# All four quarters of the expert up weights split, GpSimd forms the fourth remainder

## The chip, the cores and the metric

The kernel runs on one core of one Trainium2 chip. The metric is the device time in microseconds of one execution; a shorter time is better. Its engines are TensorE (PE in the profile, with its weight loads as PEld), VectorE (DVE), ScalarE (ACT), GpSimd (POOL) and SyncE (SP). Each runs its own list of instructions in order, and they wait for one another by semaphores.

## What is computed

Two graph layers with a dense part each, on 1250 nodes of 512 features. The change touches only the last part, a mixture of 16 experts of which each node uses 2:

```python
cw = jnp.sum(jax.nn.one_hot(idx, E) * w[..., None], axis=1)        # top-2 weights of each node
he = jnp.einsum('nd,edh->enh', xf, expert_w1) + expert_b1[:, None, :]
te = swiglu5(he, ...)                                               # clip, sigmoid, products
oe = jnp.einsum('enh,ehd->end', te, expert_w2) + expert_b2[:, None, :]
y = jnp.einsum('ne,end->nd', cw, oe)
```

`expert_w1` is 512 x 768 for each expert, `expert_w2` 384 x 512. All of it is float32.

## The kernel before

The 2500 node-expert assignments are sorted by expert and cut into **blocks** of 128 rows that belong to one expert; with this input there are 28 blocks, numbered 0 to 27. Each block b goes through these steps. Blocks come in pairs, an even one (buffer k = 0) and an odd one (k = 1), and pair i holds blocks 2i and 2i+1. Pairs 3 to 13 are a loop on every engine.

- **SP** loads the expert's weights into WB, five buffers deep, and only where the expert changes.
- **POOL** `gather` (L653, L656): copies the block's row numbers to `idx`, and an indirect DMA fetches its 128 rows into `xg[k]`. It waits until the rows of block b-2 have been transposed (`xt_ps`).
- **PE** `turn_rows` (L1356): four transposes of the gathered rows into PSUM bank 4.
- **ACT** `rows_hi`: copies the fourth quarter (128 of the 512 features) as plain float32 to `xgf` (L965), and rounds the three others to fp32r as XGH (L966). **DVE** `rows_lo` (L1998) forms their remainder XGL.
- **ACT** `split_hi` (L976), once for each half h of the 768 columns: rounds three quarters (FR = 3) of the up weights to fp32r as W1H. **DVE** `split_lo` (L2006) forms the remainder W1L of each half. The semaphore `w1_hi` counts the halves of ACT.
- **PE** `up`: for each half one float32 product for the fourth quarter (L1372, two records in the profile), and for each of the three others the three fp32r products high x high, low x high, high x low (L1378, nine records).
- **DVE** `units` and **ACT** `sigmoid` (L942): bias, clipping, the gated unit. **PE** `turn_act` (L1387) and **ACT** `turn_t` (L935): its transpose.
- **PE** `down` (L1425): three float32 products with `expert_w2`. **ACT** `result` (L951): scales the block's rows into `yo[k]`; for block b it waits until the scatter of block b-2 has landed, which read the same buffer (`scattered`).
- **POOL** `scatter` (L667, L672): a copy of the destinations, and an indirect DMA that adds the 128 rows into the output. Its copy waits for the landing of the scatter in front of it.

The order on each engine is written out by hand in `pair(i)`. PE: `turn_rows(2i)`, `down(2i-3)`, `up(2i-1)` with `turn_act(2i-2)` between its halves, `turn_rows(2i+1)`, `down(2i-2)`, `up(2i)`. ACT: `rows_hi(2i)`, `sigmoid(2i-2)`, `split_hi(2i)` half 0, `result(2i-3)`, `split_hi(2i)` half 1, `turn_t(2i-2)`, and then the same for the odd block, with `split_hi(2i+1)` half 0, `result(2i-2)`, `split_hi(2i+1)` half 1. POOL: `gather(2i)`, `scatter(2i-5)`, `gather(2i+1)`, `scatter(2i-4)`; the gathers of blocks 0 to 3 stand ahead of that, and five scatters behind the loop.

Before the experts, ACT stores the finished output rows of the shared part in three stores (`store`, the first one of HEAD node tiles), since W1H and W1L of the odd buffer lie where those rows lay.

Of the kernel before, what the change touches and what calls it, by code (L numbers as in the profile page):

```python
# [14 lines left out]
ALU = mybir.AluOpType  # L15
# [8 lines left out]
D = 512  # L24
# [3 lines left out]
FT = D // 128  # L28
# [50 lines left out]
INTER = 384  # L79
H2 = 2 * INTER  # L80
# [4 lines left out]
WBUF = O_B1 + H2  # L85
EARLY = NT
NWB = 5
# [5 lines left out]
ASSIGN = TOPK * NT  # L93
LENT = (1, 3, 5, 7)
AHEAD = 5
HEAD = 5
FR = 3
WIDE = ((0, 112), (112, NP))


def build(nc, a, out):
    ctx = ExitStack()
    with ctx:
# [3 lines left out]
        def sem(name):  # L107
            return ctx.enter_context(nc.semaphore(name))

        PS = ctx.enter_context(nc.psum_tensor("PS", [128, 8, 512], F32))  # L110
# [59 lines left out]
        f32 = lambda m: m.bitcast(F32)  # L170
# [5 lines left out]
        YF = at("YF", R_YH, [128, NT * D])  # L176
        RT = at("RT", R_YL, [128, NT * D])
        QX = at("QX", R_XN, [128, NT * D])
        WB = at("WB", R_ZH, [128, NWB * WBUF])
# [127 lines left out]
        w1_in = [sem("w1_in0"), sem("w1_in1")]  # L307
        w2_in = [sem("w2_in0"), sem("w2_in1")]
        xt_ps, xgt_ready = sem("xt_ps"), sem("xgt_ready")
        xgt_hi, xgt_f, w1_hi, w1_lo, out_head = sem("xgt_hi"), sem("xgt_f"), sem("w1_hi"), sem("w1_lo"), sem("out_head")  # L310
        hb_ready, clip_done, clip_g, gate_sig, t_gs, t_ready = (
            sem("hb_ready"), sem("clip_done"), sem("clip_g"), sem("gate_sig"), sem("t_gs"), sem("t_ready"))
        clip_u = sem("clip_u")
# [5 lines left out]
        out_stored = sem("out_stored")  # L319
# [42 lines left out]
        W1H = [at("W1H0", R_XN + 8192, [128, FR, H2], F32R), at("W1H1", R_X, [128, FR, H2], F32R)]  # L362
        W1L = [at("W1L0", R_YL + ROWB - W1B, [128, FR, H2], F32R), at("W1L1", R_X + W1B, [128, FR, H2], F32R)]
        XGH = at("XGH", R_YH + 4096, [128, 2, FR, 128], F32R)
        XGL = at("XGL", R_YL + 4096, [128, 2, FR, 128], F32R)
        xgf = YF[:, 1792:2048].rearrange("p (b n) -> p b n", b=2)

        rat = [2 * INTER]

# [43 lines left out]
        eb_i = sb("eb_i", [1, 4, NB], I32)  # L413
# [129 lines left out]
        def _(pool):  # L543
# [105 lines left out]
            def gather(i, k, b):  # L649
                if not (isinstance(b, int) and b < 2):  # L650
                    pool.wait_ge(xt_ps, b - 1)
                turn = b + 1 if isinstance(b, int) else pool.to_reg(b + 1)
                pool.tensor_copy(idx[:, k:k + 1], tok[:, bass.ds(b, 1)]).then_inc(idx_ready, 1)  # L653
                pool.wait_ge(xn_stored, 32)
                pool.wait_ge(idx_ready, turn)
                pool.indirect_dma_start(xg[:, k, :], None, xn_dram[:, :],  # L656
                                        bass.IndirectOffsetOnAxis(idx[:, k:k + 1], 0)
                                        ).then_inc(gathered[k], 16)

            def scatter(k, b):  # L660
                if isinstance(b, int):
                    turn, seen = b + 1, 16 * b
                else:
                    turn, seen = pool.to_reg(b + 1), pool.to_reg(b * 16)
                if not (isinstance(b, int) and b < 1):
                    pool.wait_ge(scattered, seen)
                pool.tensor_copy(dest_i[:, k:k + 1], home[:, bass.ds(b, 1)]).then_inc(dest_ready, 1)  # L667
                pool.wait_ge(out_head, 32)
                pool.wait_ge(out_stored, 64)
                pool.wait_ge(yo_ready, turn)  # L670
                pool.wait_ge(dest_ready, turn)
                pool.indirect_dma_start(out[:, :], bass.IndirectOffsetOnAxis(dest_i[:, k:k + 1], 0), yo[:, k, :], None,  # L672
                                        compute_op=ALU.add).then_inc(scattered, 16)

            for b in range(4):
                gather(0, b % 2, b)
            pool.wait_ge(zeroed, 16)
            last = last_pair(pool)

            def pair(i):  # L680
                gather(i, 0, i * 2)
                if not (isinstance(i, int) and i * 2 < AHEAD):
                    scatter(1, i * 2 - AHEAD)
                gather(i, 1, i * 2 + 1)
                scatter(0, i * 2 + 1 - AHEAD)

            pair(2)
            with pool.Fori(3, NB // 2) as i:
# [9 lines left out]
        def _(act):  # L698
# [66 lines left out]
            n = 0  # L765
# [196 lines left out]

            def rows_hi(k, b):
                act.wait_ge(xt_ps, b + 1)
                nc.scalar.copy(xgf[:, k, :], PS[:, 4, FR * 128:D]).then_inc(xgt_f, 1)  # L965
                nc.scalar.copy(XGH[:, k, :, :], PS[:, 4, 0:FR * 128].rearrange("p (f n) -> p f n", f=FR)  # L966
                               ).then_inc(xgt_hi, 1)

# [50 lines left out]
        def _(pe):  # L1019
# [33 lines left out]
            for b in range(NBAT):  # L1053
# [6 lines left out]
                for j in range(PER):  # L1060
# [5 lines left out]
                    for x in range(OWN):  # L1066
                        mm = nc.tensor.matmul(windows(b)[:, :, place], oh_lo[b % RING][0:CHUNK, j, :, x],  # L1067
                                              oh_key[b % RING][0:CHUNK, j, :, x].rearrange("p (t w) -> p t w", t=NT),
                                              start=False, stop=(j == PER - 1 and x == OWN - 1 and b == NBAT - 1))
# [38 lines left out]
            for t in range(NT):  # L1108
                mm = nc.tensor.matmul(PS[0:NP, 3, t:t + 1], invc[0:1, t * NP:(t + 1) * NP], ones[0:1, 0:1],
                                      start=True, stop=True)  # L1110
# [61 lines left out]
            for pos in range(POS):  # L1172
                for t in range(NT):
                    i = pos * NT + t
# [175 lines left out]
            def turn_rows(i, k, b):  # L1350
                pe.wait_ge(gathered[k], i * 16 + 16)
                if not (isinstance(b, int) and b < 1):
                    pe.wait_ge(xgt_ready, b)
                    pe.wait_ge(xgt_f, b)
                for f in range(FT):
                    mm = nc.tensor.transpose(PS[:, 4, f * 128:(f + 1) * 128], xg[:, k, f * 128:(f + 1) * 128], ident[:, :])  # L1356
                mm.then_inc(xt_ps, 1)
# [3 lines left out]
                    pe.wait_ge(clip_done, p - 1)  # L1361

            def up(k, b, between):
                off = pe.value_load(eb_i[0:1, 1, bass.ds(b, 1)], min_val=0, max_val=(NWB - 1) * WBUF)
                pe.wait_ge(xgt_f, b + 1)
                up_bank_free(b)
                for h in range(2):
                    if h and between:
                        between()
                    cols = slice(h * INTER, (h + 1) * INTER)  # L1370
                    pe.wait_ge(w1_lo, b * 2 + (h + 1))
                    nc.tensor.matmul(PS[:, 2 * k + h, 0:INTER], xgf[:, k, :],  # L1372
                                     WB[:, bass.ds(off + (FR * H2 + h * INTER), INTER)], start=True, stop=False)
                    if h == 0:
                        pe.wait_ge(xgt_ready, b + 1)
                    for f in range(FR):
                        for j, (x, wt) in enumerate(((XGH, W1H), (XGL, W1H), (XGH, W1L))):
                            mm = nc.tensor.matmul(PS[:, 2 * k + h, 0:INTER], x[:, k, f, :], wt[k][:, f, cols],  # L1378
                                                  start=False, stop=(f == FR - 1 and j == 2))
                mm.then_inc(hb_ready, 1)  # L1380

            def turn_act(k, p):
# [102 lines left out]
        def _(dve):  # L1485
# [515 lines left out]
            def split_lo(k, b, h):  # L2001
                off = dve.value_load(eb_i[0:1, 1, bass.ds(b, 1)], min_val=0, max_val=(NWB - 1) * WBUF)
                cols = slice(h * INTER, (h + 1) * INTER)
                dve.wait_ge(w1_hi, b * 2 + (h + 1))
                raw = WB[:, bass.ds(off, FR * H2)].rearrange("p (f n) -> p f n", f=FR)
                v.tensor_tensor(W1L[k][:, :, cols], raw[:, :, cols], f32(W1H[k][:, :, cols]), ALU.subtract  # L2006
                                ).then_inc(w1_lo, 1)

            def units(k, b, then):
# [204 lines left out]
```

## Time and profile before

| | us |
|---|---|
| median of 3 runs | 865.25 (862.41 to 865.94) |
| the profiled execution | 863.68 |
| its span, first to last instruction | 861.7 |
| busy in the span: PE | 792.2 (92%) |
| PE weight loads | 618.9 (72%) |
| DVE | 528.1 (61%) |
| ACT | 321.1 (37%) |
| POOL | 139.2 (16%) |

The stage of the experts runs from about 620 us of the span to its end. The profile gives each instruction's line, start and duration, which engine or DMA ended the idle time in front of it, the chain of waits that ended last, and the clock that TensorE was granted as a share of its full speed. Several records of one line are merged there, and the count is given as x4 or x9.

### The profile page before, as it was taken

The page shows a single profiled execution, that of the slowest core. Times are in us where ns is not written, and L with a number is a line of the kernel's source. Part 1 is how long each engine was busy: PE and PEld are TensorE (multiplying, and loading weights), DVE is VectorE, ACT ScalarE, POOL GpSimd, SP SyncE. Part 2 cuts the span into 40 slices and gives each one's busy share as a digit, 9 for nine tenths or more (in the row PEclk, how much of TensorE's full clock was granted, in tenths as well). Part 3 has the DMA queues.
Part 4 walks back from the last instruction along what each step waited for, and adds up shares of the span by engine and source line. Part 5 has one row for each costly group of instructions (what it writes and reads, how often), then busy time and mean ns, then how long its engine had stood idle before and what let it go on. Part 6 is the DMA issues. An engine that isn't in the chain of part 4 may idle for free.

```text
span 861.7 us, 13555 instructions
## 1 busy us (share of the span) xinstructions
PE 792.2 (92%) x3933; PEld 618.9 (72%) x3934; DVE 528.1 (61%) x943; ACT 321.1 (37%) x542; POOL 139.2 (16%) x186
## 2 busy tenths in 40 slices
PE   3899899999999989997999969988989999999983
PEld 1556788888888876676888857877867777777761
DVE  7787832421441487887023675897487878778751
ACT  1563512521431204533211253332255555556531
POOL 2000000000000210000000500212134343545321
PEclk9999899999999998998999998987999999999997
DMA  7500000000000010000101103002998949874632
GB/s 173 162 1 2 1 1 1 1 0 1 1 1 1 31 52 0 1 1 1 49 1 45 72 2 120 1 0 90 335 339 271 312 94 361 268 201 73 155 60 35
DMA packets 32292, 71.39 MB, mean 83 GB/s; under 512 B 4387, under 2 KB 4637, under 8 KB 32243
## 3 DMA queue, kind: packets, MB, share of 16 engines
q1 hardware_dynamic: 24480, 53.31, 17.8%
q0 software_dynamic: 6272, 14.68, 8.5%
q10 hardware_dynamic: 1491, 2.73, 0.9%
q8 instruction: 32, 0.52, 0.2%
q14 instruction: 17, 0.14, 0.0%
HBM read 96.53 MB, written 12.72 MB: 127 GB/s over the span
## 4 chain that ended last, share of the span: by engine, by line
PE 77%; DVE 15%; issue 4%; ACT 2%; DMA 1%; DVEq 1%; ACTq 0%; POOL 0%; POOLq 0%
PE PS L1125 22%; PE PS L1159 10%; PE PS L1378 9%; PE PS L1425 8%; PE PS L1257 5%; PE PS L1067 4%; PE PS L1372 4%; PE PS L1200 3%; PE PS L1410 3%; PE PS L1049 2%; PE PS L1356 1%; PE PS L1387 1%; PE PS L1098 1%; DVE XN L1495 1%; PE PS L1302 1%
## 5 line engine op out<-in xcount | busy, mean ns | idle before, releaser
L1125 PE MATMUL PS<-CTR,YH 125*128 125x500 f32 (+1 forms) x480 | 164.4, 358 | 2.3 <-DVE YL L1683 2.3
L1125 PE MATMUL PS<-CTR,YL 125*128 125x500 f32 (+1 forms) x480 | 163.8, 356 | 0.0
L1125 PEld LDWEIGHTS PS<-CTR,YH 125*128 125x128 f32 x480 | 91.6, 191 | 15.6 <-DVE YL L1683 2.6
L1125 PEld LDWEIGHTS PS<-CTR,YL 125*128 125x128 f32 x480 | 91.8, 191 | 13.0
L2006 DVE TENSOR_TENSOR W1L<-WB,W1H 128x1152 fp32r<-128x1152 f32 x56 | 74.0, 1356 | 17.1 <-issue 10.1
L1425 PE MATMUL PS<-WB,YF 128*128 x168 | 78.6, 605 | 2.5 <-issue 1.7
L1710 DVE TENSOR_TENSOR ZL<-PS,ZH 128x500 fp32r<-128x500 f32 (+1 forms) x36 | 21.1, 591 | 90.4 <-ACT ZH L789 90.4
L1378 PE MATMUL PS<-W1H,XGH 128*128 128x384 f32 x168 | 73.2, 436 | 0.0
L976 ACT CAST W1H<-WB 128x1152 fp32r x56 | 64.2, 1151 | 16.3 <-issue 11.0
L1378 PE MATMUL PS<-W1L,XGH 128*128 128x384 f32 x168 | 57.3, 341 | 0.0
L1378 PE MATMUL PS<-W1H,XGL 128*128 128x384 f32 x168 | 56.9, 339 | 0.0
L789 ACT CAST ZH<-PS 128x500 fp32r<-128x500 f32 (+1 forms) x36 | 18.1, 508 | 97.5 <-PE PS L1125 97.5
L672 POOL DMA_INDIRECT out<-YF,dest_i x28 | 48.3, 1727 | 35.1 <-ACT YF L951 20.2
L1425 PEld LDWEIGHTS PS<-WB,YF 128*128 128x128 f32 x168 | 30.2, 193 | 30.4 <-issue 30.4
L1372 PE MATMUL PS<-WB,YF 128*128 x112 | 45.5, 488 | 2.4 <-DVE W1L L2006 2.4
L1159 PE MATMUL PS<-WH,ZH 128*125 128x512 f32 x120 | 47.3, 394 | 0.0
L1159 PE MATMUL PS<-WL,ZH 128*125 128x512 f32 x120 | 47.3, 394 | 0.0
L1159 PE MATMUL PS<-WH,ZL 128*125 128x512 f32 x120 | 47.2, 394 | 0.0
L1067 PE MATMUL PS<-ET 125*128 125x120 f16 x330 | 44.0, 309 | 2.1 <-issue 2.1
L566 POOL MEMSET FMASK<- 128x1 f32 x1 | 0.1, 98 | 283.0 <-PE PS L1125 283.0
L1721 DVE SCALAR_TENSOR_TENSOR tmp<-PS,dis,bias 125x512 f32<-125x512 f32 x30 | 22.5, 751 | 35.7 <-PE PS L1159 35.7
L1067 PEld LDWEIGHTS PS<-ET 125*128 125x128 f16 x330 | 30.5, 135 | 18.3 <-issue 17.4
(393 smaller groups left out, 1638.9 us busy)
## 6 DMA issues: line engine op xcount, KB each, us to landing
WB<-in_w SPq DMA_DIRECT2D x28, 1536.0 KB
WB<-in_w SPq DMA_DIRECT2D x28, 768.0 KB
WB<-in_b SPq DMA_DIRECT2D x28, 384.0 KB
X<-in_x SPq DMA_DIRECT2D x1, 2240.0 KB
xn_dram<-XN SPq DMA_DIRECT2D x1, 2240.0 KB
WNEXT<-in_W SPq DMA_DIRECT2D x2, 1024.0 KB, 10.1
SR<-in_sw SPq DMA_DIRECT2D x1, 1536.0 KB, 7.7
out<-X ACTq DMA_DIRECT2D x1, 1120.0 KB
```

What stands on the lines that cost most here:

```text
L672: pool.indirect_dma_start(out[:, :], bass.IndirectOffsetOnAxis(dest_i[:, k:k + 1], 0), yo[:, k, :], None, compute_op=ALU.add).then_inc(sca ...
L976: nc.scalar.copy(W1H[k][:, :, cols], raw[:, :, cols]).then_inc(w1_hi, 1)
L1067: mm = nc.tensor.matmul(windows(b)[:, :, place], oh_lo[b % RING][0:CHUNK, j, :, x], oh_key[b % RING][0:CHUNK, j, :, x].rearrange("p (t w) ...
L1125: mm = nc.tensor.matmul(dest, lhs, rhs, start=(t == 0 and h == 0), stop=(t == NT - 1 and h == 1))
L1159: mm = nc.tensor.matmul(PS[0:NP, 6 + n % 2, :], z[:, f, t * NP:(t + 1) * NP], w[:, f, :], start=(f == 0 and h == 0), stop=(f == FT - 1 and ...
L1200: mm = nc.tensor.matmul(PS[0:TILE[j], 3 + j, 0:RC], w[rows, k, cols], x, start=(k == tiles[0] and h == 0), stop=(k == 2 and h == 2))
L1257: mm = nc.tensor.matmul(PS[:, 4 + n % 4, 0:w], wt[:, f, fo * 128:(fo + 1) * 128], z[:, f, c0:c0 + w], start=(f == 0 and h == 0), stop=(f = ...
L1372: nc.tensor.matmul(PS[:, 2 * k + h, 0:INTER], xgf[:, k, :], WB[:, bass.ds(off + (FR * H2 + h * INTER), INTER)], start=True, stop=False)
L1378: mm = nc.tensor.matmul(PS[:, 2 * k + h, 0:INTER], x[:, k, f, :], wt[k][:, f, cols], start=False, stop=(f == FR - 1 and j == 2))
L1410: nc.tensor.matmul(PS[0:NP, bank, :], x[:, c, nodes], wt[:, c, :], start=(c == 0 and j == 0), stop=False)
L1425: mm = nc.tensor.matmul(PS[:, 6 + k, :], tt[:, k, j, :], WB[:, bass.ds(off + (O_W2 + j * D), D)], start=(j == 0), stop=(j == 2))
L2006: v.tensor_tensor(W1L[k][:, :, cols], raw[:, :, cols], f32(W1H[k][:, :, cols]), ALU.subtract).then_inc(w1_lo, 1)
```

## The change

HEAD goes from 5 to 6 and FR from 3 to 4: ACT rounds all four quarters of the rows and of the weights (512 instead of 384, and 1536 instead of 1152 elements of each partition), and the separate copy `xgf` with its semaphore is gone. DVE forms the remainder of all four quarters of the rows, and of three quarters of the weights as before. The remainder of the weights' fourth quarter, 768 elements of each partition, is formed by POOL in a new step, `split_rest`, which waits for both halves of ACT's rounding of that block and raises `w1_rest`. PE replaces the float32 product by three fp32r ones and waits for `w1_rest` ahead of the last product of each half.

```diff
-HEAD = 5
-FR = 3
+HEAD = 6
+FR = FT
...
+            def split_rest(k, b):
+                off = pool.value_load(eb_i[0:1, 1, bass.ds(b, 1)], min_val=0, max_val=(NWB - 1) * WBUF)
+                pool.wait_ge(w1_hi, b * 2 + 2)
+                pool.tensor_tensor(W1L[k][:, FR - 1, :], WB[:, bass.ds(off + (FR - 1) * H2, H2)],
+                                   f32(W1H[k][:, FR - 1, :]), ALU.subtract).then_inc(w1_rest, 1)
+
             for b in range(4):
                 gather(0, b % 2, b)
+            split_rest(0, 0)
+            pool.wait_ge(out_stored, 64)
+            for b in range(1, 4):
+                split_rest(b % 2, b)
             pool.wait_ge(zeroed, 16)
...
                     scatter(1, i * 2 - AHEAD)
                 gather(i, 1, i * 2 + 1)
+                split_rest(0, i * 2)
                 scatter(0, i * 2 + 1 - AHEAD)
+                split_rest(1, i * 2 + 1)
...
             def rows_hi(k, b):
                 act.wait_ge(xt_ps, b + 1)
-                nc.scalar.copy(xgf[:, k, :], PS[:, 4, FR * 128:D]).then_inc(xgt_f, 1)
...
                     pe.wait_ge(w1_lo, b * 2 + (h + 1))
-                    nc.tensor.matmul(PS[:, 2 * k + h, 0:INTER], xgf[:, k, :],
-                                     WB[:, bass.ds(off + (FR * H2 + h * INTER), INTER)], start=True, stop=False)
...
                         for j, (x, wt) in enumerate(((XGH, W1H), (XGL, W1H), (XGH, W1L))):
+                            if f == FR - 1 and j == 2:
+                                pe.wait_ge(w1_rest, b + 1)
...
-                v.tensor_tensor(W1L[k][:, :, cols], raw[:, :, cols], f32(W1H[k][:, :, cols]), ALU.subtract
+                v.tensor_tensor(W1L[k][:, 0:FR - 1, cols], raw[:, :, cols], f32(W1H[k][:, 0:FR - 1, cols]), ALU.subtract
```

The place on POOL is the second half of a pair in the loop. Before, from the wait of the second gather to the branch back:

```order
L652 ISA [waits xt_ps]
L653 COPY idx<-tok 128x1
L656 DMA YF<-xn_dram,idx 128x512 [waits idx_ready,xn_stored]
L664 ISA
L667 ISA [waits scattered]
L667 COPY dest_i<-RT 128x1
L672 DMA out<-YF,dest_i 1378x512 [waits yo_ready,dest_ready,out_stored,out_head]
L689 UNCONDITIONAL_BRANCH
```

In the changed kernel the same gather is followed by these rows; W1L_109 is the remainder of the even buffer, W1L_110 that of the odd one, and the row behind the last is the branch back to the next pair's gather:

```order
L678 ISA [waits w1_hi]
L678 TENSOR_TENSOR W1L_109<-WB,W1H_107 128x768
L664 ISA
L667 ISA [waits scattered]
L667 COPY dest_i<-RT 128x1
L672 DMA out<-YF,dest_i 1378x512 [waits yo_ready,dest_ready,out_stored,out_head]
L676 ISA
L676 TENSOR_LOAD eb_i
L676 ISA x2
L677 ISA
L678 ISA [waits w1_hi]
L678 TENSOR_TENSOR W1L_110<-WB,W1H_108 128x768
```

Two waits for ACT's `w1_hi` now stand in POOL's list, one ahead of the second scatter and one ahead of the next pair's two gathers.

On PE the place is one half of `up`. Before:

```order
L1372 ISA [waits w1_lo,clip_done,xgt_f]
L1372 MATMUL PS<-WB,YF 128x384
L1378 MATMUL PS<-W1H_107,XGH 128x384 [waits xgt_ready]
L1378 MATMUL PS<-W1H_107,XGL 128x384
L1378 MATMUL PS<-W1L_109,XGH 128x384
L1378 MATMUL PS<-W1H_107,XGH 128x384
L1378 MATMUL PS<-W1H_107,XGL 128x384
L1378 MATMUL PS<-W1L_109,XGH 128x384
L1378 MATMUL PS<-W1H_107,XGH 128x384
L1378 MATMUL PS<-W1H_107,XGL 128x384
L1378 MATMUL PS<-W1L_109,XGH 128x384
```

And in the changed kernel:

```order
L1386 MATMUL PS<-W1H_107,XGH 128x384 [waits xgt_ready,w1_lo,clip_done]
L1386 MATMUL PS<-W1H_107,XGL 128x384
L1386 MATMUL PS<-W1L_109,XGH 128x384
L1386 MATMUL PS<-W1H_107,XGH 128x384
L1386 MATMUL PS<-W1H_107,XGL 128x384
L1386 MATMUL PS<-W1L_109,XGH 128x384
L1386 MATMUL PS<-W1H_107,XGH 128x384
L1386 MATMUL PS<-W1H_107,XGL 128x384
L1386 MATMUL PS<-W1L_109,XGH 128x384
L1386 MATMUL PS<-W1H_107,XGH 128x384
L1386 MATMUL PS<-W1H_107,XGL 128x384
L1386 MATMUL PS<-W1L_109,XGH 128x384 [waits w1_rest]
```

The float32 product is gone, twelve fp32r products stand where there were nine, and the last of them waits for POOL.

## Rows read from the trace of the kernel before

**Rows 1.** The page's chain that ended last, share of the span by engine.

```profile
PE 77%; DVE 15%; issue 4%; ACT 2%; DMA 1%; DVEq 1%; ACTq 0%; POOL 0%; POOLq 0%
```

**Rows 2.** The chain of waits over blocks 4 and 5: start us, us, what.

```profile
642.93 0.44 PE PS L1356 x4
643.37 2.58 PE PS L1425 x6
645.95 0.65 PE PS L1372 x2
646.59 1.57 PE PS L1378 x9
648.16 0.33 PE PS L1387 x3
...
650.71 0.44 PE PS L1356 x4
```

**Rows 3.** Stretches: us, busy us (and count) by engine, clock, DMA share, GB/s.

```profile
640.00:820.00 180.00, 180.00 (x814) 133.09 (x812) 144.38 (x186) 104.66 (x163) 78.71 (x89) 1.00 0.75 223
846.00:850.00 4.00, 4.00 (x6) 1.22 (x5) 0.00 (x0) 0.00 (x0) 0.59 (x2) 0.57 0.52 66
```

**Rows 4.** Timeline of POOL, 704 to 713: start, us, instruction, [idle before].

```profile
704.43 1.85 POOL L672 DMA_INDIRECT out<-YF,dest_i  x1 [0.83 <-POOL dest_i L667]
705.77 0.71 POOL L653 COPY idx<-tok 128x1 int32 x1
707.26 1.17 POOL L656 DMA_INDIRECT YF<-xn_dram,idx  x1 [0.77 <-POOL idx L653]
709.64 0.18 POOL L667 COPY dest_i<-RT 128x1 int32 x1 [1.22 <-DMA out<-YF,dest_i]
711.11 1.62 POOL L672 DMA_INDIRECT out<-YF,dest_i  x1 [1.28 <-ACT YF L951]
```

**Rows 5.** Lines L656 (gather) and L672 (scatter): their count and their landing.

```profile
L656 POOL DMA_INDIRECT YF<-xn_dram,idx x28: 967/1114/2002, 602.4 to 807.9; - x28
DMA to landing us min/median/max: 3.4/5.7/6.8
...
L672 POOL DMA_INDIRECT out<-YF,dest_i x28: 1561/1673/2173, 640.5 to 852.0; - x28
DMA to landing us min/median/max: 4.6/5.1/9.0
```

**Rows 6.** Groups by line and shape: POOL's two long subtractions, busy us, mean ns.

```profile
L614 POOL TENSOR_TENSOR SL<-SR,SH 128x3072 fp32r<-128x3072 f32 x1 | 6.8, 6831 | 0.0
L616 POOL TENSOR_TENSOR SL<-SR,SH 128x1536 fp32r<-128x1536 f32 x1 | 3.5, 3499 | 0.0
```

**Rows 7.** Timeline of ACT for block 3.

```profile
635.79 0.48 ACT L966 CAST XGH<-PS 128x384 fp32r<-128x384 f32 x1
637.13 0.65 ACT L942 ACTIVATE bias<-bias,acts 128x384 f32<-128x384 f32 x1 [0.85 <-DVE bias L2023]
637.84 1.15 ACT L976 CAST W1H<-WB 128x1152 fp32r x1
638.90 0.68 ACT L951 ACTIVATE YF<-PS,wslot 128x512 f32<-128x512 f32 x1
639.48 1.15 ACT L976 CAST W1H<-WB 128x1152 fp32r x1
```

**Rows 8.** Timeline of POOL and DVE in the shared part, around 556 and 560.

```profile
556.11 1.26 POOL L643 TENSOR_TENSOR TL<-ST,TH 128x500 fp32r<-128x500 f32 x1 [12.66 <-ACT TH L915]
556.95 0.96 DVE L1942 SCALAR_TENSOR_TENSOR ST<-SG,SC,ST 128x500 f32<-128x500 f32 x1
...
560.25 0.78 DVE L1942 SCALAR_TENSOR_TENSOR ST<-SG,SC,ST 128x500 f32<-128x500 f32 x1
```

**Rows 9.** Timeline of the last block: its down product, its scatter.

```profile
845.73 4.53 PE L1425 MATMUL PS<-WB,YF 128*128 x6 [0.72 <-ACT YF L935]
...
852.00 1.57 POOL L672 DMA_INDIRECT out<-YF,dest_i  x1 [1.94 <-ACT YF L951]
```

More of the change, by code:

```diff
@@ L309, in build @@
         xt_ps, xgt_ready = sem("xt_ps"), sem("xgt_ready")
-        xgt_hi, xgt_f, w1_hi, w1_lo, out_head = sem("xgt_hi"), sem("xgt_f"), sem("w1_hi"), sem("w1_lo"), sem("out_head")
+        xgt_hi, w1_hi, w1_lo, out_head = sem("xgt_hi"), sem("w1_hi"), sem("w1_lo"), sem("out_head")
+        w1_rest = sem("w1_rest")
         hb_ready, clip_done, clip_g, gate_sig, t_gs, t_ready = (
@@ L365, in build @@
         XGL = at("XGL", R_YL + 4096, [128, 2, FR, 128], F32R)
-        xgf = YF[:, 1792:2048].rearrange("p (b n) -> p b n", b=2)
         rat = [2 * INTER]
@@ L1353, in turn_rows @@
                     pe.wait_ge(xgt_ready, b)
-                    pe.wait_ge(xgt_f, b)
                 for f in range(FT):
@@ L1363, in up @@
             def up(k, b, between):
-                off = pe.value_load(eb_i[0:1, 1, bass.ds(b, 1)], min_val=0, max_val=(NWB - 1) * WBUF)
-                pe.wait_ge(xgt_f, b + 1)
                 up_bank_free(b)
@@ L1377, in up @@
                         for j, (x, wt) in enumerate(((XGH, W1H), (XGL, W1H), (XGH, W1L))):
+                            if f == FR - 1 and j == 2:
+                                pe.wait_ge(w1_rest, b + 1)
                             mm = nc.tensor.matmul(PS[:, 2 * k + h, 0:INTER], x[:, k, f, :], wt[k][:, f, cols],
-                                                  start=False, stop=(f == FR - 1 and j == 2))
+                                                  start=(f == 0 and j == 0), stop=(f == FR - 1 and j == 2))
                 mm.then_inc(hb_ready, 1)
@@ L2004, in split_lo @@
                 dve.wait_ge(w1_hi, b * 2 + (h + 1))
-                raw = WB[:, bass.ds(off, FR * H2)].rearrange("p (f n) -> p f n", f=FR)
-                v.tensor_tensor(W1L[k][:, :, cols], raw[:, :, cols], f32(W1H[k][:, :, cols]), ALU.subtract
+                raw = WB[:, bass.ds(off, (FR - 1) * H2)].rearrange("p (f n) -> p f n", f=FR - 1)
+                v.tensor_tensor(W1L[k][:, 0:FR - 1, cols], raw[:, :, cols], f32(W1H[k][:, 0:FR - 1, cols]), ALU.subtract
                                 ).then_inc(w1_lo, 1)
```

## The prediction

> **What bounds the kernel now.** I read the page's chain first: 77% of the span lies on PE [rows 1]. Then the chain over two blocks of the stage that the change touches [rows 2]. It is PE without a gap: four transposes 0.44, the down product 2.58, a half of `up` 0.65 + 1.57, the transposes of the activation 0.33, and the other half 0.65 + 1.57. From one block's transposes to the next one's are 650.71 − 642.93 = 7.78 us. The stage's sums say the same: PE is busy for all of 180 us at full clock, DVE for 144 and ACT for 105 of them [rows 3]. So the stage is bound by PE, and everything else must only be in time. The reader should then ask how much in time POOL is, since the change gives it new work with new waits. POOL's timeline [rows 4] has the gather of block b start 1.7 us behind the end of the transposes of block b−2 (642.93 + 8 × 7.78 + 0.44 = 705.6, then 707.26), and its landing takes 5.7 us by the median [rows 5]. The rows are needed 15.56 − 0.44 = 15.1 us after they were allowed to be fetched, so POOL may be 15.1 − 1.7 − 5.7 = 7.7 us later than now before PE waits.
>
> **PE's part.** A half of `up` loses the float32 product, 0.65, and gains three fp32r products at 1.57/9 = 0.174 each, 0.52: 0.13 less for each half, 0.25 for each block, 7 us for 28 blocks. PE's period becomes 7.53. That is what the change brings if PE stays the bound.
>
> **ACT's and DVE's part.** ACT's cast of 384 elements takes 0.48 and that of 1152 takes 1.15 [rows 7], 0.87 ns an element, so the two casts of a block take 1.48 instead of 1.15, and that of the rows 0.59. The copy `xgf` goes. ACT gains about half a microsecond a block and DVE 0.1, and both have over 1.5 us of idle time a block [rows 3]; as work this costs nothing. But the end of the second cast now releases POOL. HEAD moves one tile of output from the second store into the first: the same bytes, taken as nothing, with 1 us either way.
>
> **POOL's part.** `split_rest` subtracts 768 elements. POOL's two long subtractions give (6831 − 3499)/1536 = 2.17 ns an element [rows 6], 1.67, and 0.08 behind ACT's semaphore: 1.75 us. As work that would fit beside the 79 us in 180 of now. What matters is the wait. `split_rest(2i+1)` stands ahead of the branch back, so ahead of `gather(2i+2)`, and it waits for ACT to round block 2i+1, which ACT starts only when PE has transposed the rows of 2i+1. But PE needs `gather(2i+2)` just one period after that. So the gather loses all its lead: what was issued a period ahead is now issued when the block in front is half done.
>
> I follow the loop from A, the end of the transposes of block 2i, all in us:
>
> 1. ACT: rounds the rows, then (rows 7 for the starts: 637.13 to 637.84 is 0.71, to 638.90 is 1.06) the sigmoid, half 0 and `result(2i−3)`. It would reach that at 0.05 + 0.52 + 0.71 + 1.06 + 0.33 = 2.7 (the 0.52 is the 0.59 less its overlap with the next). But the down product in front of it runs on a PE that has waited for many microseconds. After the waits at the end of the program the granted clock was 0.57 of the full 2.4 GHz, so mostly at the level of 1.2 GHz, and this same down took 4.53 [rows 3, 9]. So `result` starts at 4.5, half 1 at + 0.58, and ends at + 1.48: **6.6**.
> 2. POOL: `split_rest(2i)`, **1.75**.
> 3. POOL: `scatter(2i−4)`: the copy and its wait 1.0 [rows 4], and the landing: median 5.1, largest 9.0 [rows 5]. Weight loads are issued behind each `down`, thus about now, and I take 6.3: **7.3**. Its landing counts since ACT's `result(2i−2)` waits for it, and half 1 of the odd block stands behind that `result`. By here A + 15.6 is reached. PE's way to the same point: 4.4 (cold down) + 2 × 2.09 + 0.33 + 0.44 = 9.4 to the next transposes, and ACT 3.6 to `result`: 13.0. So the scatter is later, not PE.
> 4. ACT: `result` and half 1: 0.15 + 0.58 + 1.48 = **2.2**.
> 5. POOL: `split_rest(2i+1)`, **1.75**.
> 6. POOL: `gather(2i+2)`: copy 0.18, then 0.76 until the DMA [rows 4], the landing 3.4 to 6.8 [rows 5]; the queues are rather quiet at this point, so below the median: 4.4. Four transposes take 0.44 warm and twice that at half the clock, 0.8: **6.15**.
>
> The sum is 6.6 + 1.75 + 7.3 + 2.2 + 1.75 + 6.15 = 25.75 us for a pair, where now it is 15.56. The gather of 2i+1 is issued behind one scatter and is in time (about A + 4 against A + 9).
>
> **The whole.** Block 3: its transposes end at 635.6 and ACT's second cast at 640.6 [rows 7], now 0.66 later, and `split_rest(3)` ends at 643.05. Then `gather(4)`, here beside weight loads (5.7 instead of 4.4): the transposes of block 4 end at 650.5 instead of 643.4. Eleven pairs later, block 26: 650.5 + 11 × 25.75 = 933.7. Steps 1 to 5 follow once more (19.6) to 953.3; then five scatters in a row, each 1.0 + 5.1, since only now POOL comes to them: the last one's DMA starts 0.3 (reading the loop's end, an estimate) + 1.0 + 4 × 6.1 later, at 979.0. In the profile 9.7 us lie between that point and the end [rows 9], so the span is 988.7. The profiled execution is 2.0 above its span, 863.68, and the median of the runs 1.6 above it: 992 us. That the 7 us on PE don't show is part of this: PE waits 8 to 9 us in each pair (25.75 − 0.8 − 9.4 − 7.1).
>
> **The bounds of the unknown costs.** Below: a landing of 3.4 for the gather and 4.6 for the scatter and no loss of clock: 4.95 + 1.75 + 5.6 + 2.2 + 1.75 + 4.95 = 21.2 a pair, 942 in all. Above: landings of 5.7 and 9.0 and the rival on the port below in full: 25.75 + 1.3 + 2.7 + 2.7 = 32.5, 1066 in all. All at one end is unlikely.
>
> **The rivals.**
>
> *POOL and DVE hold each other up.* `split_rest` and the DVE's `split_lo` of half 1 wait for the same semaphore. In the shared part, a DVE instruction with two inputs from SBUF took 0.96 when it began under a subtraction of POOL, and 0.78 otherwise [rows 8]. If the DVE's 1.36 goes first, POOL starts 1.35 later, twice a pair: 28.45, and 11 × 2.7 = 30 us more, 1022. For it: both engines are idle and waiting there. Against it: POOL started 0.08 behind ACT in the shared part, the DVE about 0.16, and where POOL goes first it is DVE that waits, which costs nothing. 20%. The Trainium skill, SBUF — State Buffer, section "Who interferes with whom", states the rule: such a DVE instruction and a GpSimd instruction that reads SBUF exclude each other, and whichever is first holds the port for its whole length. The 0.18 us of the rows agrees with that, but shows only DVE as the one that waits.
>
> *The scatter is off the chain.* If it lands before PE's way arrives (within 3.7 us of its issue, under the least of 4.6, or with PE colder for longer), the pair is 9.4 + 3.6 + 0.58 + 1.48 + 1.75 + 6.15 = 22.95, and the time 961. 12%.
>
> *PE stays the bound, the change is faster.* It needs `gather(2i+2)` issued within the 7.7 us of slack. The last step ahead of it must then end 7.53 − 0.44 − 0.94 − 5.7 = 0.45 us after the odd block's transposes. The time would be 865 − 7 = 858. For it: PE is the only bound now, and POOL has the time as a sum. Against it: ACT's second cast alone ends 640.6 + 0.66 − 635.6 = 5.7 us after those transposes, and the list of POOL leaves no other way around. 3%.
>
> **The chances.** The loop as written 62%, the port 20%, the scatter off the chain 12%, PE bound 3%, and 3% for something else, a part of it near the time of now. Faster by over 0.5% (which is what a measurement of this kernel can tell from no change) 3%, within it 1%, slower 96%. The range for 8 in 10: the loop with landings about a microsecond off either way is 11 × 2 = 22 on either side, the two neighbouring cases lie at 961 and 1022: 950 to 1045.
>
> **What would show it.** In the profile after: PE idle for 8 to 9 us ahead of every even block's transposes from block 4 on, and the wait ends by the gather's DMA; the clock below 1.00 behind each of these waits; POOL's `split_rest` behind idle time that ACT's cast ended; ACT's `result` of the even blocks waiting for the scatter's DMA; the `up` halves at 12 × 0.174 = 2.09; 24 to 28 us between the transposes of blocks 2i and 2i+2; POOL's subtraction at 1.7, and at 3 where the port decides. The prediction is wrong if PE runs through, or if the gather of an even block starts ahead of the casts of the block in front of it.

## The result, and the profile after

| | before | after |
|---|---|---|
| median of 3 runs | 865.25 us | 1016.25 us (1015.67 to 1018.85) |
| profiled execution / its span | 863.68 / 861.7 us | 1016.25 / 1014.5 us |
| mean granted clock of PE | 0.967 | 0.903 |

The changed kernel takes 1.178 times as long [1.1755, 1.1806]: 151 us more. 992 us was predicted, in a range of 950 to 1045.

The page's chain that ended last, of the changed kernel (share of the span by engine), stands against [rows 1]:

```profile
PE 56%; DVE 12%; DMA 12%; issue 11%; ACT 5%; POOLq 1%; POOL 1%; ACTq 1%; SPq 0%; DVEq 0%
```

PE falls from 77% to 56%; DMA goes from 1% to 12%, and "issue" from 4% to 11%. The stage was PE without a gap [rows 2]; now its chain runs over DMAs. The same chain over one pair of blocks (start us, us, what; the short pieces between these are left out) shows its links:

```profile
707.24 1.11 PE PS L1366 x4
708.42 4.47 PE PS L1433 x6
713.07 0.30 ACT YF L963
713.79 1.49 ACT W1H L987
715.66 2.76 issue
718.42 0.19 POOL dest_i L667
719.42 5.92 DMA out<-YF,dest_i
725.45 0.29 ACT YF L963
726.16 1.48 ACT W1H L987
728.41 2.33 issue
730.74 0.19 POOL idx L653
731.72 3.40 DMA YF<-xn_dram,idx
735.24 1.11 PE PS L1366 x4
```

The links are, in order: cold transposes and a cold down product on PE (cold means at a lowered clock), ACT's `result` and cast, a hole of 2.76, POOL's scatter, ACT's `result` and cast again, a hole of 3.1 (727.64 to 730.74), POOL's gather, and PE. From transposes to transposes are 28.0 us, where two blocks took 15.56 before [rows 2]. The holes are POOL's `split_rest`, of which the chain names only 0.09 and calls the rest "issue"; the timelines of DVE and POOL do (start, us, instruction, [idle before and what ended it]):

```profile
715.42 1.36 DVE L2014 TENSOR_TENSOR W1L<-WB,W1H 128x1152 fp32r<-128x1152 f32 x1 [1.99 <-ACT W1H L987]
715.46 3.02 POOL L678 TENSOR_TENSOR W1L<-WB,W1H 128x768 fp32r<-128x768 f32 x1 [6.13 <-ACT W1H L987]
...
727.77 1.36 DVE L2014 TENSOR_TENSOR W1L<-WB,W1H 128x1152 fp32r<-128x1152 f32 x1 [4.46 <-ACT W1H L987]
727.81 2.98 POOL L678 TENSOR_TENSOR W1L<-WB,W1H 128x768 fp32r<-128x768 f32 x1 [6.78 <-ACT W1H L987]
```

Both engines waited for the same cast, DVE begins 0.04 ahead, and POOL's 768 elements take 3.0, not 1.75. The line's group has it for all blocks (min/median/max ns):

```profile
L678 POOL TENSOR_TENSOR W1L<-WB,W1H x28: 1845/2994/3022, 615.7 to 976.0; 128x768 fp32r<-128x768 f32 x28
```

The view of waits from 620 to the end (engine and line, what it waited for: total us, times, longest) reads the same way from the other side:

```profile
POOL W1L L678 <- ACT W1H L987: 174.1, 27, 8.7
...
PE PS L1366 <- DMA YF<-xn_dram,idx: 117.1, 12, 11.6
...
ACT YF L963 <- DMA out<-YF,dest_i: 43.5, 13, 4.8
```

PE loses 117.1 us in twelve waits for the gather of an even block, 10.3 in the one ahead of 735.24, and more by its clock. Of the stretches (us, busy us and count of PE, PEld, DVE, ACT, POOL, clock, DMA share, GB/s) the first answers to [rows 3], the second is the down product behind such a wait:

```profile
660.00:820.00 160.00, 96.96 (x405) 70.91 (x403) 72.21 (x91) 58.29 (x66) 67.47 (x58) 0.80 0.52 150
708.40:712.80 4.40, 4.38 (x7) 1.98 (x8) 2.66 (x4) 2.68 (x3) 0.93 (x1) 0.63 0.48 106
```

PE is busy 61% where it was busy all the time, no other engine is above 46%, and the DMA engines are at 52%: nothing is the bound by its work.

### The profile page after: what moved, and what is told of

Same layout as the page of the kernel before. It is cut to its first block, busy times and chain, and to the rows that moved or that the text cites. A ratio compares the mean times of both kernels' runs of the same rounds, so it can differ in the third digit from the quotient of the medians.

```text
span 1014.5 us, 13638 instructions
## 1 busy us (share of the span) xinstructions
PE 817.3 (81%) x3989; PEld 639.6 (63%) x3990; DVE 535.0 (53%) x943; ACT 342.5 (34%) x514; POOL 207.7 (20%) x215
## 4 chain that ended last, share of the span: by engine, by line
PE 56%; DVE 12%; DMA 12%; issue 11%; ACT 5%; POOLq 1%; POOL 1%; ACTq 1%; SPq 0%; DVEq 0%
PE PS L1136 18%; PE PS L1170 8%; DMA out<-YF,dest_i 7%; PE PS L1433 6%; PE PS L1268 4%; DMA YF<-xn_dram,idx 4%; PE PS L1078 4%; ACT W1H L987 4%; PE PS L1386 3%; PE PS L1211 3%; PE PS L1418 2%; PE PS L1366 2%; PE PS L1060 1%; PE PS L1109 1%; DVE XN L1503 1%
## 5 line engine op out<-in xcount | busy, mean ns | idle before, releaser
L1366 PE MATMUL PS<-ident,YF 128*128 128x128 f32 x112 | 23.4, 346 | 117.1 <-DMA YF<-xn_dram,idx 117.1
L678 POOL TENSOR_TENSOR W1L<-WB,W1H 128x768 fp32r<-128x768 f32 x28 | 81.7, 2919 | 174.3 <-ACT W1H L987 174.1
L1433 PE MATMUL PS<-WB,YF 128*128 x168 | 99.9, 741 | 4.1 <-ACT YF L947 3.0
L1386 PE MATMUL PS<-W1H,XGH 128*128 128x384 f32 x224 | 90.2, 402 | 1.4 <-DVE W1L L2014 1.4
L987 ACT CAST W1H<-WB 128x1536 fp32r x56 | 82.4, 1477 | 15.3 <-issue 9.4
L1386 PE MATMUL PS<-W1L,XGH 128*128 128x384 f32 x224 | 76.7, 342 | 0.0
L1386 PE MATMUL PS<-W1H,XGL 128*128 128x384 f32 x224 | 76.1, 340 | 0.0
L2006 DVE TENSOR_TENSOR XGL<-PS,XGH 128x512 fp32r<-128x512 f32 x28 | 19.3, 688 | 63.0 <-ACT XGH L977 61.1
L672 POOL DMA_INDIRECT out<-YF,dest_i x28 | 45.3, 1618 | 23.2 <-POOL dest_i L667 22.4
L1386 PEld LDWEIGHTS PS<-W1H,XGH 128*128 128x128 f32 x224 | 43.5, 194 | 8.4 <-issue 6.8
L1386 PEld LDWEIGHTS PS<-W1H,XGL 128*128 128x128 f32 x224 | 43.3, 193 | 6.6 <-issue 6.6
```

What stands on the lines that cost most here:

```text
L678: pool.tensor_tensor(W1L[k][:, FR - 1, :], WB[:, bass.ds(off + (FR - 1) * H2, H2)], f32(W1H[k][:, FR - 1, :]), ALU.subtract).then_inc(w1_r ...
L987: nc.scalar.copy(W1H[k][:, :, cols], raw[:, :, cols]).then_inc(w1_hi, 1)
L1433: mm = nc.tensor.matmul(PS[:, 6 + k, :], tt[:, k, j, :], WB[:, bass.ds(off + (O_W2 + j * D), D)], start=(j == 0), stop=(j == 2))
```

## The experiments

Ratios are against the kernel before, run on the same chip (its medians were 863.6 to 864.6).

**1. The waits alone.** The kernel before, with nothing but the two waits in POOL's list:

```diff
                 gather(i, 1, i * 2 + 1)
+                pool.wait_ge(w1_hi, (i * 2) * 2 + 2)
                 scatter(0, i * 2 + 1 - AHEAD)
+                pool.wait_ge(w1_hi, (i * 2 + 1) * 2 + 2)
```

> The kernel before with nothing but two waits added to POOL's list in pairs 2 to 13, at the places where the changed kernel has its subtractions: for both halves of ACT's cast of block 2i ahead of the second scatter, and of block 2i+1 ahead of the branch back. No subtraction on POOL, no other cast, the float32 product stays. Theory (the waits, not the work, are the larger part): the gather of each even block is issued behind the cast of the block in front, PE waits ahead of it, the pair takes 20 to 21.5 us instead of 15.6, and the time is 920 to 945 us, about 935. That is roughly half of the loss of 151 us; the rest is 2 x 3.0 us of subtraction and the longer casts, which only count because they lie on this chain. Rival (a wait alone costs nothing while POOL has the time as a sum): 865 us.

Measured: 971.57 us (967.72 to 975.23), ratio 1.125 [1.1202, 1.1289]. Two waits with no work behind them cost 108 of the 151 us. That is the mechanism, but dearer than I expected: the pair shown below is 716.58 to 740.20, 23.6 us, and from block 6 to block 26 a pair takes 25.1 in the mean. POOL's timeline, with DVE and PE beside it, tells part of why:

```profile
725.06 1.36 DVE L2008 TENSOR_TENSOR W1L<-WB,W1H 128x1152 fp32r<-128x1152 f32 x1 [2.31 <-ACT W1H L978]
725.17 1.29 POOL L667 COPY dest_i<-RT 128x1 int32 x1 [6.54 <-ACT W1H L978]
...
735.02 0.77 POOL L653 COPY idx<-tok 128x1 int32 x1 [6.14 <-ACT W1H L978]
...
740.20 1.09 PE L1358 MATMUL PS<-ident,YF 128*128 128x128 f32 x4 [4.80 <-DMA YF<-xn_dram,idx]
```

The copy of one element a partition takes 1.29 when DVE's subtraction begins ahead of it, and ends 0.04 behind it; with DVE out of its way it takes 0.18 [rows 4] or 0.20, and 0.71 to 0.77 where it begins under a scatter's issue. The gather's copy of 0.77 above ends 0.05 behind another subtraction of DVE (734.38 to 735.74). PE then waits 4.8, and its record of four transposes is 1.09 long, where a warm one has 0.60 (of which 0.44 pass before the down product begins). The chain over this pair shows two more links that my expectation didn't name:

```profile
717.75 5.11 PE PS L1427 x6
...
727.29 4.98 DMA out<-YF,dest_i
```

They are the cold down product and the landing of the scatter, which also waits for a cast here.

**2. DVE behind POOL.** The changed kernel; DVE's half 1 waits for POOL's remainder of that block, so the two are never at it together.

```diff
+                if h and not (isinstance(b, int) and b < 2):
+                    dve.wait_ge(w1_rest, b + 1)
```

> The changed kernel, but DVE's subtraction of half 1 waits until POOL's subtraction of the same block is done (blocks 2 and later), so the two never overlap at that point. Theory (the port: DVE goes first for 1.36 us and POOL starts behind it): POOL's subtraction falls from 2.99 to 1.7 us, twice in each pair on the chain, the pair from about 28.0 to 25.4 us, the time by 26 x 1.3 = 33 us, to about 984 us. Rival (POOL's subtraction takes 2.99 us by itself with these operands, with or without DVE): 2.99 us stays and the time stays at 1016 us or above.

Measured: 997.79 us (996.71 to 1002.79), ratio 1.157 [1.1532, 1.1604]: 18 us less than the changed kernel, not 33. The duration of the term is settled by the line's group:

```profile
L678 POOL TENSOR_TENSOR W1L<-WB,W1H x28: 1792/1830/2047, 615.7 to 956.8; 128x768 fp32r<-128x768 f32 x28
```

1.83 for the same instruction on the same data, where the changed kernel has 2.99. The Trainium skill, SBUF — State Buffer, section "Who interferes with whom", has the rule for this: a DVE instruction with two inputs from SBUF and a GpSimd instruction that reads SBUF exclude each other, and the first one holds on for its whole length; here 1.16 us are added to the one that comes second, by a DVE instruction of 1.36. Pairs lie between 24.8 and 27.6, 26.1 in the mean, where I expected 25.4. The view of waits from 620 to 1000 has what changed beside POOL:

```profile
ACT bias L954 <- DVE bias L2033: 33.1, 14, 3.5
ACT YF L963 <- DMA out<-YF,dest_i: 3.1, 5, 1.4
```

ACT's wait for DVE's clip was 15.2 in the changed kernel, and its wait for the scatter 43.5: DVE comes later by its new wait. The chain over the pair from 701.46 to 728.45 has, beside that, a longer cold down product and a longer landing of the gather than the changed kernel's pair (4.47 and 3.40):

```profile
702.64 5.42 PE PS L1433 x6
...
724.30 4.02 DMA YF<-xn_dram,idx
```

How the missing 15 us divide between these isn't shown.

**3. The scatter ahead of the first remainder.** The changed kernel with two calls exchanged.

```diff
                 gather(i, 1, i * 2 + 1)
-                split_rest(0, i * 2)
                 scatter(0, i * 2 + 1 - AHEAD)
+                split_rest(0, i * 2)
                 split_rest(1, i * 2 + 1)
```

> The changed kernel with the pair's second scatter moved ahead of the first remainder in POOL's list, so it no longer waits for the cast of block 2i. Theory (the scatter's landing is a link of the chain, since ACT's result and behind it the second half of the odd block's cast wait for it): ACT's wait for the scatter goes, PE's way to the same point takes over 2 to 4.5 us earlier, the pair falls from about 28.0 to about 24 us, the time by 11 x 4.4 = 48 us, to about 968 us (960 to 990). Rival (the gather's lateness alone sets the pair, the scatter runs beside PE): no change, 1016 us.

Measured: 979.59 us (976.59 to 981.52), ratio 1.133 [1.1294, 1.1362]. ACT's wait for the scatter is all but gone,

```profile
ACT YF L963 <- DMA out<-YF,dest_i: 2.3, 2, 1.7
```

and a pair takes 24.7 in the mean from block 4 to block 26 (the shortest is 725.36 to 748.81, 23.5), where the changed kernel has 27.8. So the scatter behind the first remainder was a link of the chain (steps 2 and 3 of the prediction). That the way over PE is what remains in its place was expected, and isn't shown apart.

**4. Both casts ahead of `result`.** The changed kernel; in ACT's list `split_hi(i, 0, ..., 1)` stands ahead of `result(1, i*2−3)`, and the odd one likewise:

```diff
                 split_hi(i, 1, i * 2 + 1, 0)
-                result(0, i * 2 - 2)
                 split_hi(i, 1, i * 2 + 1, 1)
+                result(0, i * 2 - 2)
```

> The changed kernel itself (1016 us) with only ACT's order changed: both halves of the cast ahead of the result. POOL's list keeps its waits. Theory (the chain runs through down, result and the scatter's landing into the second half of the cast): w1_hi comes at about 4.2 instead of 6.9 us behind the transposes of an even block, the scatter's landing is no longer awaited ahead of the odd block's cast, and the pair falls to about 23.4 us: 965 us (955 to 985), with the gathers of even blocks still behind POOL's wait. Rival (only POOL's order matters): 1016 us.

Measured: 975.87 us (975.31 to 977.52), ratio 1.130 [1.125, 1.1339], within the 955 to 985 expected, with pairs of 24.4 in the mean: the cast that releases POOL no longer stands behind the cold down product and the scatter's landing. ACT's wait for the scatter falls from 43.5 to 11.4. Experiments 3 and 4 each take most of ACT's wait for the scatter away, and each leaves 111 to 116 us of the loss, near what the waits alone cost: the gather of the even block still stands behind the second cast of the block in front of it.

**5. The gathers ahead of the remainders.** Each pair forms the remainders of the two blocks in front of it, each behind one of its gathers and one of its scatters:

```diff
-            for b in range(1, 4):
-                split_rest(b % 2, b)
+            split_rest(1, 1)
...
                     scatter(1, i * 2 - AHEAD)
+                split_rest(0, i * 2 - 2)
                 gather(i, 1, i * 2 + 1)
-                split_rest(0, i * 2)
                 scatter(0, i * 2 + 1 - AHEAD)
-                split_rest(1, i * 2 + 1)
+                split_rest(1, i * 2 - 1)
...
                 scatter((j + 1) % 2, end + j)
+                if j < 2:
+                    split_rest(j, end + 3 + j)
```

> The changed kernel with POOL's list shifted: in pair i it forms the remainders of blocks 2i-2 and 2i-1 instead of 2i and 2i+1, each behind the gather of two blocks later, so that no gather stands behind a wait for the cast of the block in front of it. All of POOL's work stays, 28 subtractions. Theory (the order of the waits is the whole loss): PE runs without a gap again at 7.53 us a block instead of 7.78, gathers start about 1.7 us behind the transposes that free their buffer, and the time is 865 - 7 = 858 us (855 to 861). Rival (POOL's work and its hold on the port are the loss, 28 x 3.0 us of subtraction beside DVE): most of the loss stays, the time is over 930 us. Between: if the DVE, held up by POOL, comes too late with its half of the weights, PE has a short wait in each block and the time is 862 to 880.

Measured: 888.41 us (885.47 to 890.99), ratio 1.028 [1.0255, 1.0305]. All arithmetic of the change is still there, and the larger `HEAD` too, and 128 of the 151 us are gone: so much of the loss is one of order. But it is not faster than the kernel before. In the stretch of 160 us PE is idle for 15.6:

```profile
660.00:820.00 160.00, 144.39 (x667) 111.91 (x666) 128.19 (x145) 89.32 (x107) 101.14 (x91) 0.97 0.64 181
```

The timelines of POOL and DVE show one place:

```profile
688.75 1.60 POOL L672 DMA_INDIRECT out<-YF,dest_i  x1 [0.83 <-POOL dest_i L667]
689.82 2.40 POOL L678 TENSOR_TENSOR W1L<-WB,W1H 128x768 fp32r<-128x768 f32 x1
```

```profile
689.31 3.14 DVE L2032 TENSOR_SCALAR bias<-bias,clampv 128x384 f32<-128x384 f32 x1 [0.19 <-DVE bias L2029]
```

DVE's clip of 384 elements takes 0.48 elsewhere. Here it begins under POOL's issue of a scatter and ends at 692.45, 0.23 behind the end of POOL's subtraction; its mean is 1.05 from 641 to 840. The clip stands on the way to the next down product.

**6. DVE forms all four quarters.** POOL's list is that of before.

```diff
-                split_rest(0, i * 2)
-                split_rest(1, i * 2 + 1)
...
-                            if f == FR - 1 and j == 2:
-                                pe.wait_ge(w1_rest, b + 1)
...
-                raw = WB[:, bass.ds(off, (FR - 1) * H2)].rearrange("p (f n) -> p f n", f=FR - 1)
+                raw = WB[:, bass.ds(off, FR * H2)].rearrange("p (f n) -> p f n", f=FR)
```

> The changed kernel with the fourth quarter's remainder formed by DVE together with the others (1536 elements of each partition in each half instead of 1152), POOL's list as in the kernel before, no wait on POOL in PE's products. Theory (the waits in POOL's list are the loss): PE bound, 858 us. DVE gains 2 x 0.4 us a block and is busy for about 7.1 of 7.53 us; if its order leaves gaps at that load, PE waits a little and the time is up to 870. Rival (POOL's work costs): also fast, so this run alone does not part them. Rival (twelve fp32r products or the longer casts of ACT are the loss): stays near 1016.

Measured: 875.99 us (872.39 to 877.98), ratio 1.015 [1.0125, 1.0168]. The full computation of the change without POOL is the nearest to the kernel before. The stretch shows DVE at 137.5 of 160 us, 86% (80% in [rows 3]):

```profile
660.00:820.00 160.00, 150.26 (x719) 115.53 (x718) 137.53 (x156) 98.51 (x118) 75.86 (x80) 1.00 0.66 186
```

From block 6 on, blocks take 7.9 to 8.7 us, 8.3 in the mean, where 7.78 is to be beaten. That DVE's load is what holds them up is argued from its share, not shown.

**7. The gathers ahead, with a remainder of 32 columns.** As experiment 5, but POOL subtracts 32 columns instead of 768; the fourth quarter's product with the remainder uses `W1H` in its place, so that remainder is left out of the result.

```diff
-                pool.tensor_tensor(W1L[k][:, FR - 1, :], WB[:, bass.ds(off + (FR - 1) * H2, H2)],
-                                   f32(W1H[k][:, FR - 1, :]), ALU.subtract).then_inc(w1_rest, 1)
+                pool.tensor_tensor(W1L[k][:, FR - 1, 0:32], WB[:, bass.ds(off + (FR - 1) * H2, 32)],
+                                   f32(W1H[k][:, FR - 1, 0:32]), ALU.subtract).then_inc(w1_rest, 1)
```

> The kernel with the shifted list of POOL (888 us in its run), where POOL subtracts only 32 of the 768 elements of the fourth quarter, and PE takes the rounded weights instead of their remainder in the last of the twelve products: the remainder of the fourth quarter is left out of the result. All instructions, waits and products otherwise stay. Theory (what the shifted order still loses is the port: POOL's subtraction holds up DVE's clips for 1 to 2.7 us each): the clips are back at 0.48 us, PE runs without a gap at about 7.53 us a block, and the time is 858 us (856 to 863). Rival (the twelve products make ACT's longer casts and DVE's chain the bound whatever POOL does): it stays at 875 to 888.

Measured: 874.64 us (873.46 to 876.43), ratio 1.013 [1.0103, 1.0148]. The 856 to 863 of the theory is missed, and the time is that of the rival. POOL's subtraction was worth 14 us (888.41 to 874.64); with it nearly gone there is still nothing of PE's 7 us. The timeline of DVE and ACT over one block:

```profile
691.77 0.96 DVE L2031 TENSOR_TENSOR YF<-PS,WB 128x768 f32<-128x768 f32 x1 [0.97 <-issue]
693.68 0.64 ACT L955 ACTIVATE YF<-YF,acts 128x384 f32<-128x384 f32 x1 [2.59 <-DVE YF L2034]
694.53 1.48 ACT L988 CAST W1H<-WB 128x1536 fp32r x1 [0.21 <-issue]
695.91 0.68 ACT L964 ACTIVATE YF<-PS,wslot 128x512 f32<-128x512 f32 x1
696.49 1.47 ACT L988 CAST W1H<-WB 128x1536 fp32r x1
698.11 1.36 DVE L2017 TENSOR_TENSOR W1L<-WB,W1H 128x1152 fp32r<-128x1152 f32 x1 [0.55 <-ACT W1H L988]
699.75 0.96 DVE L2031 TENSOR_TENSOR bias<-PS,WB 128x768 f32<-128x768 f32 x1 [0.28 <-issue]
```

It is a ring: DVE's bias and clips, ACT's sigmoid, cast, `result`, cast, then DVE's subtraction, and the next bias stands behind that. One turn is 699.75 − 691.77 = 7.98 us. With casts of 1.15 [rows 7] it would be 0.65 shorter, 7.3 (an estimate; no run has it), under PE's 7.78; with casts of 1.48 it is above PE's 7.53. The ring isn't all: from block 6 on the blocks take 8.4 in the mean, some over 9.

**8. The same, both casts ahead of `result`.** The lists of experiment 7, with the exchange of experiment 4.

> The kernel of the run at 875 us (shifted order, 32 of 768 elements subtracted by POOL, the remainder of the fourth quarter left out of the result), and now ACT does both halves of the cast ahead of the result of the older block instead of around it. Theory (a ring of DVE and ACT is what holds that kernel at about 8.0 us a block: bias 0.96, clip 0.5, sigmoid 0.65, cast 1.48, result 0.6, cast 1.48, DVE's second subtraction 1.36 and the gaps; with casts of 1.15 as before it was 7.3 and hidden under PE's 7.78): the result leaves the ring, which falls to 7.4, PE at 7.53 is the bound and the time is 858 us (856 to 863). Rival (DVE's own work and gaps are the bound): no change, 875.

Measured: 868.78 us (865.19 to 870.18), ratio 1.0048 [1.0026, 1.007]: above the 856 to 863 expected. The ring is shorter by `result`, and PE's own period shows up in the timeline of its transposes:

```profile
632.56 0.60 PE L1367 MATMUL PS<-ident,YF 128*128 128x128 f32 x4
...
640.10 0.60 PE L1367 MATMUL PS<-ident,YF 128*128 128x128 f32 x4
...
647.65 0.60 PE L1367 MATMUL PS<-ident,YF 128*128 128x128 f32 x4
```

7.54 and 7.55, against 7.53 of the prediction. Not all blocks are so: four take 9.0 to 9.7, and the mean from block 6 on is 8.0. In the stretch from 660 to 820 PE is idle for 6.6 us, and nearly all of it is a wait for POOL's small subtraction:

```profile
PE PS L1389 <- POOL W1L L678: 6.1, 5, 1.9
```

It comes late because it stands behind a copy that waited for a scatter's landing:

```profile
729.57 0.34 POOL L667 COPY dest_i<-RT 128x1 int32 x1 [3.77 <-DMA out<-YF,dest_i]
```

So the ring was a part of what held experiment 7: without `result` in it 5.9 us of the 17 expected came back. The rest is in the main this second wait, as far as the view shows.

**9. Three that missed.** Half each: POOL forms the remainder of half 1 alone, DVE that of half 0.

```diff
-                pool.tensor_tensor(W1L[k][:, FR - 1, :], ...
+                pool.tensor_tensor(W1L[k][:, FR - 1, INTER:], ...
...
-                raw = WB[:, bass.ds(off, (FR - 1) * H2)].rearrange("p (f n) -> p f n", f=FR - 1)
+                raw = WB[:, bass.ds(off, (FR - h) * H2)].rearrange("p (f n) -> p f n", f=FR - h)
```

> The shifted order with the fourth quarter's remainder shared: POOL forms that of half 1 only (384 elements), DVE that of half 0 with its own three. Nothing is left out. Theory: POOL holds the port for 0.85 us instead of 1.7 a block, DVE gains 0.4 us instead of 0.8: between the two ways that took 888 and 876, and if the two costs do not add up, a little below both, 868 to 880. It is not expected to fall under the 864 of the kernel before, since DVE is then busy or held up for about 7.8 us a block. Rival (either cost alone is what hurts, and half of each fits): 858 to 862, faster than before.

Measured: 883.66 us (881.83 to 888.34), ratio 1.023 [1.0204, 1.0253].

Experiment 5 with the exchange of experiment 4 (the full remainder):

> A full version, nothing left out: the shifted order of POOL (888 us) with both halves of ACT's cast ahead of the result. Theory: the ring is shorter by 0.6 us, but POOL's subtraction of 1.7 us still holds up DVE's clips once in each block; 870 to 882 us, between 858 and 888. Rival (the ring alone made the 888): 858 to 862.

Measured: 898.22 us (896.79 to 902.54), ratio 1.040 [1.0368, 1.0438]: slower than experiment 5. A later `result` makes the scatter later; in the waits from 660 to 820 of this kernel

```profile
POOL out L672 <- ACT YF L964: 33.8, 14, 3.0
```

stands against 18.4 in experiment 5, and the subtraction behind it moves with it. It meets DVE's clip more often: the clip's mean from 641 to 840 is 2.23 in the one buffer and 1.68 in the other, where experiment 5 has 1.05 in both.

The same with POOL's subtraction cut into four pieces of 192 columns:

> The same with POOL's subtraction in four pieces of 192 elements. Theory (a DVE instruction waits for the POOL instruction that holds the port to end): the longest hold falls from 1.7 to 0.45 us, so DVE loses less in each block, and POOL's pieces wait between DVE's instead: below the run with one piece, 862 to 875 us. Rival (the port changes hands at each piece and DVE waits for every one): as slow as with one piece or slower.

Measured: 894.05 us (887.34 to 898.56), ratio 1.034 [1.0293, 1.038]. The intervals of the two ratios overlap; pieces bring little or nothing, where 862 to 875 was expected.

No version beats the kernel before.

## Why the prediction was right or wrong

The direction and the mechanism were right: PE stops being the bound, since `split_rest(2i+1)` stands ahead of `gather(2i+2)` in POOL's list. But the case that came was the neighbouring one, the loop with POOL held up by DVE (20%, 1022), and not the loop as written (62%, 992). The pair from the end of one even block's transposes, 708.35, to the end of the next one's, 736.35:

| step | predicted | measured |
|---|---|---|
| 1 ACT to the second cast | 6.6 | 6.9 (to 715.27) |
| 2 `split_rest(2i)` | 1.75 | 3.2 |
| 3 scatter and its landing | 7.3 | 6.9 (to 725.34) |
| 4 `result`, half 1 | 2.2 | 2.3 |
| 5 `split_rest(2i+1)` | 1.75 | 3.15 |
| 6 gather, transposes | 6.15 | 5.6 |
| pair | 25.75 | 28.0 |

- **Steps 2 and 5 are the term that was mis-sized.** I took 1.75 each, from 2.17 ns an element, and put the hold-up by DVE in a rival at 20%. It came in 26 of 28 blocks, as that rival had it: 3.0. My reason against it, that POOL reacts to ACT's semaphore sooner than DVE, did not hold: in the pair above POOL begins 0.19 behind the end of the cast, not 0.08, and DVE 0.15. Experiment 2 shows the term by itself: 1.83 without the overlap. So of the 1.45 that step 2 lacked, 1.2 are the overlap, and the rest is a subtraction and a wait that were each taken 0.1 to 0.2 too short.
- **The sum of 992 against 1016.25.** From block 4 to block 26 the pair was 27.84 in the mean ((956.52 − 650.26)/11), 2.1 more than predicted, 23 us in all; the start was 0.9 later, the way from block 26 to the end 56.9 instead of 55.0, and the time lies 1.75 above the span where 3.3 was added. 23.0 + 0.9 + 1.9 − 1.55 = 24.25. It is that near also because errors cancel: in the pair of the table steps 2 and 5 were 2.85 short, and steps 3 and 6 together 0.95 long.
- **Step 1** was right with its cold down: 4.47 against 4.53 [rows 9], at a clock of 0.63. Other pairs have 3.9 to 5.5, so the close fit is in part luck of the pair. **Step 3** was right in kind; experiment 3 shows that the landing was on the chain. The two `up` halves take 2.09 each, as worked out. **Step 6** was 0.6 high: the landing of 3.40 was below the 4.4 taken, the cold transposes at 1.11 above the 0.8.
- **The rival "the scatter is off the chain"** (961) needed a landing within 3.7; it was 5.9, and ACT waited 43.5 us for scatters.
- **"PE stays the bound", 858,** was rightly at 3%, but its price was too low. Experiment 7 gave it POOL's order and next to no work and had 874.64. The step behind it, that of ACT's longer casts "as work this costs nothing" because of idle time in [rows 3], was wrong where PE is the bound: those casts lie in a ring over DVE, which takes 8.0 a turn in experiment 7 and would be 7.3 with the short casts, and experiment 8 gets 5.9 us back by shortening it. In the changed kernel this isn't what decides, as the gather is later still.
- **Where the 151 us are.** The two waits alone are 108 (experiment 1). The other 43 contain the two subtractions behind them and longer casts. These don't add up as they stand: the subtractions are 2 × 3.2 a pair, and the mean pair grows only from 25.1 to 27.8, in part since without them POOL's copies stood behind DVE instead. The shares weren't measured apart from one another.

## What to carry to other kernels

An engine that issues gathers in its list's order must not get a wait for this block's compute ahead of the next block's gather: the free time that the profile shows for the engine says nothing about the lead that the gather loses. A share of idle time doesn't price a longer instruction either; follow the ring in which it stands, once around, and compare it with the period of the bound. And when two engines wait for one semaphore and then read SBUF at once, price each of them as the second.

## What the runs showed of the hardware

- DVE and POOL at the same semaphore: from block 3 on DVE's subtraction of 1152 (1.36 us) began 0.02 to 0.05 ahead every time in the changed kernel, and POOL's took 2.99 instead of 1.83 (experiment 2).
- A POOL copy of one element a partition took 1.29 behind DVE's subtraction, 0.18 to 0.20 with DVE out of its way, and 0.71 to 0.77 under a scatter's issue (experiment 1). In the trace of the kernel before one took 0.96 and ended 0.04 behind DVE's subtraction too.
- The hold-up went the other way too: a DVE clip of 384 elements with one input tensor took 3.14 instead of 0.48 beside POOL's scatter issue and the subtraction behind it (experiment 5). I had expected it of two-input instructions alone.
- After about 10 us without work PE's record of four transposes was 1.11 long (0.60 warm) and the down product took 4.47 (2.58 warm), at a granted clock of 0.63 of 2.4 GHz, thus mostly at 1.2 GHz. Over the other pairs the same cold down product took 3.9 to 5.5.
